# The four taps of a depthwise convolution: ScalarE multiplies, GpSimd adds, VectorE has no part, and the timetable is drawn up again

## The reference, cut to what matters

```python
h = x * rsqrt(mean(x * x) + EPS) * norm_scale
xs, res = split(h @ w_in, 2)
xs = silu(depthwise_conv(xs, conv_w) + conv_b)   # 4 taps, causal
delta, B, C = split(xs @ w_xproj, ...)
delta = softplus(delta @ w_dt + b_dt)
# scan over time for each of 16 states: h = exp(delta * A) * h + (delta * xs) * B
out = (y + xs * D) * silu(res)
```

## Time and profile before

| | us |
|---|---|
| median of 3 runs | 2735.68 |
| lowest and highest | 2731.32, 2737.05 |
| span of the profiled execution | 2733.1 |
| VectorE busy | 2470.7 (90%) |
| TensorE busy | 2233.0 (82%) |
| ScalarE busy | 1718.4 (63%) |
| GpSimd busy | 1638.1 (60%) |

### The profile page before, as it was taken

One profiled execution on the slowest core, in us unless ns is written; L12 is line 12 of the kernel. 1 busy time (PEld: TensorE's weight loads), 2 busy tenths in 40 slices (PEclk: granted clock), 3 DMA queues, 4 the chain that ended last, 5 costly groups with the idle time before them and its releaser, 6 DMA issues.

```text
span 2733.1 us, 35478 instructions
## 1 busy us (share of the span) xinstructions
PE 2233.0 (82%) x9268; PEld 1316.2 (48%) x9268; DVE 2470.7 (90%) x3315; ACT 1718.4 (63%) x3353; POOL 1638.1 (60%) x1083
## 2 busy tenths in 40 slices
PE   5666788888888888888888888888888888888798
PEld 2434355454544545454454545445454554545454
DVE  1699999999999999999999999999999999999951
ACT  3554675858567584766758476675847667584544
POOL 0667575757657575665757566575756757575610
PEclk9766899999999999999899998999999999999998
DMA  5011100101001010110101010010101001010100
GB/s 123 24 43 31 42 25 28 51 28 51 29 20 55 28 52 24 51 32 21 56 26 53 24 51 29 24 55 24 55 25 51 28 24 55 24 47 28 35 1 16
DMA packets 83410, 101.81 MB, mean 37 GB/s; under 512 B 23481, under 2 KB 49873, under 8 KB 83169
## 3 DMA queue, kind: packets, MB, share of 16 engines
q1 hardware_dynamic: 83168, 99.06, 12.2%
HBM read 90.13 MB, written 8.91 MB: 36 GB/s over the span
## 4 chain that ended last, share of the span: by engine, by line
DVE 37%; issue 27%; PE 14%; POOL 11%; ACT 5%; DVEq 1%; POOLq 0%; ACTq 0%
DVE h L1252 13%; DVE yT L1268 11%; PE bank L709 9%; POOL bx L680 7%; PE stateT L878 3%; DVE xs L1127 3%; DVE prod L1227 2%; ACT decay L1084 2%; ACT cum_sb L1049 2%; DVE res L1148 1%; DVE yT L1265 1%; POOL x_back L646 1%; DVE xs L1142 1%; PE bank L853 1%; DVE st L1107 1%
## 5 line engine op out<-in xcount | busy, mean ns | idle before, releaser
L680 POOL TENSOR_TENSOR bx<-dx,B_rows 128x1024 f32<-128x1024 f32 x512 | 1219.5, 2389 | 495.6 <-DVE h L1252 468.7
L1252 DVE TENSOR_TENSOR_SCAN h<-decay,bx 128x512 f32<-128x512 f32 x1024 | 1238.3, 1209 | 75.8 <-ACT decay L1084 52.0
L1084 ACT ACTIVATE decay<-delta,decay_rate 128x512 f32<-128x512 f32 x1024 | 706.8, 693 | 656.6 <-DVE h L1252 631.6
L878 PE MATMUL stateT<-ident,h 128*128 128x128 f32 x4096 | 683.6, 298 | 322.0 <-DVE h L1252 175.8
L878 PEld LDWEIGHTS stateT<-ident,h 128*128 128x128 f32 x4096 | 499.0, 150 | 725.5 <-issue 353.4
L1268 DVE SCALAR_TENSOR_TENSOR yT<-stateT,C_tok,yT 128x512 f32<-128x512 f32 x960 | 696.0, 725 | 16.3 <-PE stateT L878 16.0
L709 PE MATMUL bank<-q_to_expert,xnT 128*128 128x512 f32 x512 | 267.3, 649 | 12.5 <-ACT dx L988 12.4
L709 PE MATMUL bank<-k_to_expert,cumT 128*128 128x512 f32 x512 | 266.7, 647 | 9.3 <-DVE prod L1227 9.2
L709 PE MATMUL bank<-hT,w_in_sb 128*128 128x512 f32 x512 | 245.7, 610 | 18.1 <-DVE xs L1127 17.2
L1049 ACT ACTIVATE cum_sb<-bank,gate 128x64 f32<-128x64 f32 x1024 | 222.8, 329 | 39.4 <-PE bank L709 28.3
L853 PE MATMUL bank<-expert_to_out,prodT 128*128 128x256 f32 x1024 | 242.1, 379 | 0.4 <-ACT prodT L1059 0.4
(11 more groups left out here) (161 smaller groups left out, 2493.1 us busy)
## 6 DMA issues: line engine op xcount, KB each, us to landing
B_rows<-B_scratch SPq DMA_DIRECT2D x256, 256.0 KB, 3.2
x_front<-in_L_attn_x SPq DMA_DIRECT2D x16, 512.0 KB, 4.5
x_back<-in_L_attn_x SPq DMA_DIRECT2D x16, 512.0 KB, 5.1
out<-x_back SPq DMA_DIRECT2D x16, 512.0 KB, 3.3
w_in_sb<-in_L_attn_w_in SPq DMA_DIRECT2D x1, 1024.0 KB, 5.7
h<-in_L_ffn_V_fwd SPq DMA_DIRECT2D x2, 256.0 KB
h<-in_L_ffn_W_inv_exp SPq DMA_DIRECT2D x2, 256.0 KB
h<-in_L_ffn_W_fwd SPq DMA_DIRECT2D x2, 256.0 KB
```

What stands on the lines that cost most here:

```text
L680: pool.tensor_tensor(bx[use % BX_RING][:, :, :], dx[q.parity][:, 2 * half:2 * half + 2, :], row, ALU.mult).then_inc(s_bx.step(f"{n},{half} ...
L878: last = pe.transpose(stateT[j % 2][:, c * P:(c + 1) * P], h[n % 2][:, c, j * P:(j + 1) * P], ident[:, :])
L1084: act.activation(decay[c % 2][:, :], delta[q.parity][:, c, :], ACT.Exp, scale=decay_rate[:, c, n:n + 1]).then_inc(s_exp.step(f"{n},{c}"), 1)
L1252: dve.tensor_tensor_scan(h[n % 2][:, c, :], decay[c % 2][:, :], bx[(2 * n + c // 2) % BX_RING][:, c % 2, :], 0.0, ALU.mult, ALU.add).then_ ...
```

## The change

The three VectorE taps are gone. ScalarE, after its first product with the bias, writes three more products out of the same bank into `scratch` (task `tap`, at the same beats as `xs`), in a ring of four tiles: product p >= 4 waits for the addition of product p - 4. GpSimd adds them to `xs[c]` one after another (task `cv`, 12 additions a sequence, beats 38, 41, 43 and 52). The bank is free after the third product. The users of `scratch` and SiLU wait for GpSimd's last addition. The timetable is drawn up again; the rows below are those that move most or that the text names.

```diff
 TIMETABLE = {
-    ("F", "ag", "dve"): (8,),
-    ("F", "rs", "pool"): (15,),
-    ("F", "h", "act"): (17,),
-    ("F", "hT", "pe"): (17, 26),
-    ("F", "hT", "act"): (28, 31),
+    ("F", "ag", "dve"): (7,),
+    ("F", "rs", "pool"): (18,),
+    ("F", "h", "act"): (19,),
+    ("F", "hT", "pe"): (20, 28),
+    ("F", "hT", "act"): (29, 30),
-    ("F", "xs", "pe"): (32, 35, 37, 40),
+    ("F", "xs", "pe"): (29, 32, 34, 37),
     ("F", "xs", "act"): (34, 36, 40, 43),
-    ("F", "cvA", "dve"): (35, 37, 38, 42),
-    ("F", "cvB", "dve"): (37, 37, 39, 42),
-    ("F", "cvC", "dve"): (37, 37, 39, 44),
-    ("F", "res", "pe"): (36, 38, 41, 65),
+    ("F", "tap", "act"): (34, 36, 40, 43),
+    ("F", "cv", "pool"): (38, 41, 43, 52),
+    ("F", "res", "pe"): (35, 41, 41, 65),
...
-    ("B", "u", "dve"): (263, 264, 264, 268),
-    ("B", "o", "dve"): (268, 270, 271, 271),
-    ("B", "wo", "pe"): (274, 278, 282, 287),
-    ("B", "r", "dve"): (283, 283, 287, 289),
+    ("B", "u", "dve"): (263, 264, 267, 268),
+    ("B", "o", "dve"): (268, 268, 269, 270),
+    ("B", "wo", "pe"): (278, 280, 282, 287),
+    ("B", "r", "dve"): (284, 287, 288, 289),
...
     ("B", "rb", "pool"): (300,),
-    ("B", "t", "act"): (302,),
+    ("B", "t", "act"): (301,),
     ("B", "x1", "dve"): (301,),
...
-    ("B", "rb1", "pool"): (309,),
+    ("B", "rb1", "pool"): (314,),
...
-    ("L", "rs", "pool"): (473,),
+    ("L", "rs", "pool"): (468,),
...
-                return {"hT": (f_act, f"hT{k}"), "xs": (f_dve, f"cvC{k}"), "res": (f_act, f"res{k}"),
+                return {"hT": (f_act, f"hT{k}"), "xs": (f_act, f"tp{k}3"), "res": (f_act, f"res{k}"),
...
+            def conv_task(b, c, use):
+                pool.wait_ge(f_act.sem, f_act.done(b, f"cv{c}"))
+                for back in range(1, TAPS):
+                    product = 3 * c + back - 1
+                    pool.wait_ge(f_act.sem, f_act.done(b, f"tp{c}{back}"))
+                    if back > 1:
+                        pool.wait_ge(f_pool.sem, f_pool.done(b, f"cv{c}{back - 1}"))
+                    pool.tensor_tensor(xs[b.parity][:, c, back:], xs[b.parity][:, c, back:], scratch[:, product % 4, 0:T - back],
+                                       ALU.add).then_inc(f_pool.step(f"cv{c}{back}"), 1)
...
+            def tap_task(b, c, use):
+                act.wait_ge(f_pe.sem, f_pe.done(b, f"xs{c}"))
+                for back in range(1, TAPS):
+                    product = 3 * c + back - 1
+                    if product >= 4:
+                        before = product - 4
+                        act.wait_ge(f_pool.sem, f_pool.done(b, f"cv{before // 3}{before % 3 + 1}"))
+                    elif product == 0 and b.shift(-1).exists:
+                        act.wait_ge(f_dve.sem, f_dve.done(b.shift(-1), "d13"))
+                        if b.shift(-3).exists:
+                            act.wait_ge(b_pe.sem, b_pe.done(b.shift(-3), "lg"))
+                    act.activation(scratch[:, product % 4, 0:T - back], use.bank[:, 0:T - back], ACT.Copy,
+                                   scale=conv_w_sb[:, c, TAPS - 1 - back:TAPS - back]).then_inc(f_act.step(f"tp{c}{back}"), 1)
...
             def silu_task(b, k, use):
-                act.wait_ge(f_dve.sem, f_dve.done(b, "cvC3"))
+                act.wait_ge(f_pool.sem, f_pool.done(b, "cv33"))
...
-            def tap(back, name, before):
-
-                def task(b, c, use):
-                    x_c = xs[b.parity][:, c, :]
-                    dve.wait_ge(before[0].sem, before[0].done(b, f"{before[1]}{c}"))
-                    dve.scalar_tensor_tensor(out=x_c[:, back:], in0=use.bank[:, 0:T - back], scalar=conv_w_sb[:, c, TAPS - 1 - back:TAPS - back],
-                                             in1=x_c[:, back:], op0=ALU.mult, op1=ALU.add).then_inc(f_dve.step(f"{name}{c}"), 1)
-                return task
...
             def keep_task(b, k, use):
+                dve.wait_ge(f_pool.sem, f_pool.done(b, "r1"))
```

More of the change, by code:

```diff
@@ L104 @@
     ("F", "proj", "pe"): (75,),
[L105 to L106 removed]
+    ("F", "proj", "act"): (78,),
+    ("F", "B", "sp"): (70,),
     ("F", "Ct", "pe"): (94,),
[L108 removed]
+    ("F", "Ct", "act"): (98,),
     ("F", "dt", "pe"): (82, 89, 100, 108),
[L110 to L111 removed]
+    ("F", "dt", "act"): (90, 93, 107, 115),
+    ("F", "ex", "act"): (91, 94, 107, 117),
     ("F", "ln", "act"): (92, 96, 107, 119),
@@ L128 @@
     ("B", "ag1", "dve"): (304,),
-    ("B", "rb1", "pool"): (309,),
-    ("B", "xn", "act"): (310,),
+    ("B", "rb1", "pool"): (314,),
+    ("B", "xn", "act"): (316,),
     ("B", "xnT", "pe"): (317, 319),
-    ("B", "xnT", "act"): (320, 320),
-    ("B", "cum", "dve"): (322, 324),
+    ("B", "xnT", "act"): (320, 322),
+    ("B", "cum", "dve"): (322, 322),
     ("B", "rt", "pe"): (324, 327, 329, 333),
-    ("B", "rt", "act"): (331, 332, 332, 338),
+    ("B", "rt", "act"): (326, 328, 331, 337),
     ("B", "gelu", "act"): (338,),
-    ("B", "logit", "pe"): (342,),
@@ L138 @@
[L138 to L149, removed]
+    ("B", "logit", "pe"): (340,),
+    ("B", "logit", "act"): (344,),
+    ("B", "logit_rows", "pe"): (342,),
@@ L150 @@
+    ("B", "lb", "dve"): (344,),
+    ("B", "mx", "dve"): (345,),
+    ("B", "sub", "dve"): (345,),
+    ("B", "ex", "act"): (346,),
+    ("B", "sm", "dve"): (347,),
+    ("B", "sn", "dve"): (349,),
+    ("B", "rc", "dve"): (350,),
+    ("B", "wa", "dve"): (352,),
+    ("B", "gT", "pe"): (370,),
+    ("B", "gT", "act"): (377,),
     ("L", "cum", "pe"): (348, 354, 363, 374, 386, 390, 398, 428),
-    ("L", "xv", "pe"): (351, 358, 367, 378, 394, 423, 426, 431),
+    ("L", "xv", "pe"): (355, 358, 367, 378, 394, 423, 426, 431),
@@ L152 @@
     ("L", "cum", "act"): (357, 360, 368, 379, 391, 392, 408, 432),
[3 rows of a table removed]
[3 rows of a table added]
     ("L", "out", "pe"): (373, 381, 393, 398, 431, 434, 439, 443),
-    ("L", "out", "act"): (382, 401, 440, 445),
+    ("L", "out", "act"): (386, 401, 443, 445),
     ("L", "st", "dve"): (454,),
     ("L", "ag", "dve"): (462,),
-    ("L", "rs", "pool"): (473,),
-    ("L", "t", "act"): (468,),
-    ("F", "dx", "pool"): (105, 113, 126, 127),
+    ("L", "rs", "pool"): (468,),
+    ("L", "t", "act"): (470,),
+    ("F", "dx", "pool"): (105, 110, 126, 127),
@@ L163 @@
     ("L", "x", "pool"): (477, 477),
-    ("L", "store", "sp"): (466,),
+    ("L", "store", "sp"): (464,),
 }
-FILLED_BY = {("F", "hT"): "hT", ("F", "xs"): "xs", ("F", "cvA"): "xs", ("F", "cvB"): "xs", ("F", "cvC"): "xs", ("F", "res"): "res",
+FILLED_BY = {("F", "hT"): "hT", ("F", "xs"): "xs", ("F", "tap"): "xs", ("F", "res"): "res",
              ("F", "proj"): "proj", ("F", "Ct"): "Ct", ("F", "dt"): "dt", ("B", "u"): "y", ("B", "r"): "wo", ("B", "xnT"): "xnT",
@@ L731, in res_task @@
             def res_task(b, c, use):
+                if c == 0:
+                    pe.wait_ge(f_act.sem, f_act.done(b, "hT1"))
+                    if use.sem is f_act.sem:
+                        pe.sem_inc(passed["pe"], 1)
                 pe.wait_ge(use.sem, use.free_at)
@@ L1013, in rt_task @@
                         act.wait_ge(f_dve.sem, f_dve.done(b.shift(1), "d13"))
+                    if b.shift(2).exists:
+                        act.wait_ge(f_pool.sem, f_pool.done(b.shift(2), "cv33"))
                 act.wait_ge(b_pe.sem, b_pe.done(b, f"rt{k}"))
@@ L1084, in scan_part @@
                 act.activation(decay[c % 2][:, :], delta[q.parity][:, c, :], ACT.Exp, scale=decay_rate[:, c, n:n + 1]).then_inc(s_exp.step(f"{n},{c}"), 1)
-            walk(act, "act", prologue, {("F", "h"): h_task, ("B", "t"): t_task, ("B", "xn"): xn_task, ("L", "t"): out_centre, ("F", "hT"): hT_task, ("F", "xs"): xs_task, ("F", "res"): res_task, ("F", "silu"): silu_task,
+            walk(act, "act", prologue, {("F", "h"): h_task, ("B", "t"): t_task, ("B", "xn"): xn_task, ("L", "t"): out_centre, ("F", "hT"): hT_task, ("F", "xs"): xs_task, ("F", "tap"): tap_task, ("F", "res"): res_task, ("F", "silu"): silu_task,
                                  ("F", "proj"): proj_task, ("F", "Ct"): Ct_task, ("F", "dt"): dt_task, ("F", "ex"): ex_task, ("F", "ln"): ln_task, ("B", "xnT"): xnT_task, ("B", "rt"): rt_task,
```

20 lines of the change are left out of this document (9 added, 11 removed), and 6 rows, old and new, of the table TIMETABLE.

## The result

The changed kernel takes 2637.19 us (median of 4 runs, 2632.95 to 2640.34) where the kernel before, on the same chip, takes 2735.01 (2731.32 to 2737.05): a ratio of 0.9645, 95% interval 0.963 to 0.9659. It is faster by 97.8 us, more than twice the 40 us forecast, and lies 3 us under the low end of the range. The profiled execution has a span of 2638.5 us against 2733.1.

The account below looks back on a forecast made before the run. VectorE's own work bounds the steady period, plus 3.4 us of waits. Per period 8.06 + 2.4 - 7.35 = 3.1 us, 40 us over thirteen periods, total -40: median 2695 us (-1.5%), range 2640 to 2748.

Parts of the forecast that it names:

- The taps: Twelve taps of a sequence leave VectorE in beats 35 to 44, worth 8.06 us a period.
- The relief of `o_task`: Beats 12 to 15: with `rs` behind a `bx`, VectorE's four products get 2.4 us cheaper a period; bounds 0 and 2.7.
- The relief fails: Rival, chance 0.24: `o_task` still meets a `bx`; 0.7 us a period, 2727 us, near no change.
- the new wait: VectorE waits up to `x1` (beat 45): 7.35 us a period, near bounds 6.2 and 8.5.
- the chain up to `x1`: Slots 3 to 5: nine GpSimd additions, `bx`, `rb`, then ScalarE's `t` delay `x1` from 23.9 to 30.1, 6.2 us.
- the collision of `x1`: Beat 45: `x1` may have to wait for GpSimd's next `bx`, losing 2.3 us; half counted, 1.15.
- the price of the addition: One 512-element addition on GpSimd takes 1.35 us; bounds 1.27 and 1.70.
- The places of the waits: Beats 31 and 37 wait 1.3 and 3.0 us for TensorE, beat 44's scan for `bx`; longest wait at `x1` on `t`.
- The rest is nothing: Elsewhere the timetable moves by a beat or two, counted as nothing; 3.4 us of old waits stay.
- TensorE at half its clock: Rival, chance 0.19: `wo` 1, `wo` 2 and `xs` 0 run at 1.2 GHz, 1.7 us more each; 2762 us.
- Mostly hidden: Rival, chance 0.15: only TensorE limits in slots 3 to 5, wait 2.5 us, 8.0 gained a period; 2632 us.
- The early periods: First scanned period wins nothing, second 1.5 us; ahead of the first scan GpSimd's additions end some 1.5 us later.

Follow-up runs that it names:

- experiment 1: Changed kernel with only `rs` on GpSimd put back from beat 18 to 15, ahead of its `bx`: 2676.61 us, ratio 0.9789.
- after: The changed kernel itself, with the taps on ScalarE and GpSimd and the new order: 2637.19 us, ratio 0.9645.
- Experiment 12: Changed kernel with second `hT`, its copies and first `xs` earlier, third block's additions and fourth `xs` later, one `res` moved to beat 60: 2632.64 us.
- experiment 5: Changed kernel with half of the `xs` and `res` matmuls left out: 2611.24 us, ratio 0.9547.
- Experiment 13: Changed kernel with only the router's steps put back on the beats of the kernel before: 2640.27 us, ratio 0.965.
- experiment 3: Changed kernel's new order with the three tap steps back on VectorE at their old beats: 2759.49 us, ratio 1.0094.
- experiments 4 to 6: Changed kernel with two of three additions a block left out (2625.38 us), half the `xs` and `res` matmuls left out (2611.24), both cuts together (2550.68).

## Why the prediction came out too small

**What bounds.** Right that a microsecond taken from VectorE counts only while the others follow. VectorE's busy time fell to 2273 us, under the 2300 to 2340 forecast, mostly by the router's products.

**The taps.** 8.06 us forecast, 8.07 measured.

**The relief of `o_task`.** 2.4 forecast, 2.63 measured, and `rs` behind the `bx` did what was said (mean near 0.7: 0.677). *The relief fails* is out. Its worth was underrated all the same: experiment 1 loses 39 us, since TensorE is held up too and one `wo` runs at a lower clock.

**The step that failed: the new wait, 7.35 us in the sum and 4.84 measured.** It had two parts, the chain up to `x1` (6.2) and the collision of `x1` (1.15), and both were too large.

**The chain: the price of the addition.** I took 1.35 us for each of nine, with 1.27 as the lower bound. Three in a row take 3.57 from start to start (1191.43 to 1195.00), 1.19 each, below the lower bound. The single steps are 1.35, 1.17 and 1.04. So 1.35 was right for the first, which the second waits for; the second and third are 1.09 long where no addition of before was under 1.25, and that is 1.1 us of the nine; and the instruction behind the third does not wait for it, which is the rest. The earlier trace rows had another trap. The mean of 1.38 is no price of an addition alone:

```profile
L636 POOL TENSOR_TENSOR scratch<-scratch,dx x64: 1257/1274/1827, 70.7 to 2459.4; 128x512 f32<-128x512 f32 x64
```

The three numbers are least, median and most: 49 of the 64 take 1.29 us or less, 15 take 1.59 to 1.83, and in after, at other moments, the same addition has a mean of 1.28.

The Trainium skill, GPSIMD Engine Reference, section 3.1, gave 1.12 as an estimate of its figure; the mean of all 192 is 1.149, so the page was nearer than the rows I had, partly by luck, since no 512-element addition of this trace is that short. Its section 4.1 leaves elementwise work to VectorE; the price agrees in direction (1.19 for the addition alone where VectorE's whole tap took 0.67), but as advice it doesn't hold for this kernel, where GpSimd had the time. Nine additions are 1.4 us shorter than counted. They started at 9.4 instead of 9.2, the third block waited 0.43 us for its products, and VectorE's own work up to `x1` was 24.35 instead of 23.9 us. So `x1` starts at 29.2 instead of 30.1, and the wait is 4.84 instead of 6.2.

**The collision of `x1`.** 1.15 us counted as half a loss; the loss was nought, because `x1` came 0.13 us before the second `bx`, and GpSimd waited. That was luck: the prediction could not tell. Experiment 12 shows the loss to be real in another order: 1.2 us.

**The places of the waits.** Forecast at beats 31 and 37 for TensorE, 1.3 and 3.0: measured 1.53 and 1.60, and 0.48 later. `x1` on `t`: there, but 1.24 us and not the longest. The wait of the scan of beat 44 on `bx` did not come: the `bx` ended at 1207.25, the scan started at 1207.48. TensorE had held VectorE back just enough, and experiment 5, which frees TensorE, brings that wait out at 2.06 us.

**"The rest is nothing".** Not right: a term put at nothing. The router's products and `keep` gave 2.24 us, `gate` 0.21, other waits took 0.94 and small lengthenings 0.85, which leaves 0.66 a period. Experiment 13 shows that the products' 2.0 us are worth no time: the waits answer to them.

**TensorE at half its clock.** It did not happen to the three tasks named. The granted clock averages 0.57 in the window, lower than the 0.65 of before, but it fell on small work: two `stateT` tasks take 1.11 us instead of 0.60, a transpose of `x_front` 1.06, and the first two `wo` have 1.96 and 1.89. TensorE's gaps ahead of them were 1.12, 0.52 and 1.12 us. It was the order that spared the large tasks: in experiment 1 the first `wo` took 2.73 us, and in experiment 3 two large tasks took 3.50 and 3.41 instead of 1.88, behind gaps of 3.47 and 3.48 us and at clocks of 0.57 and 0.59. The Trainium skill, TensorE: Matmul & The Clock Gate, section "Why this matters for your kernels", warns of idle gaps between bursts of matmuls; the trace of experiment 3 agrees.

```profile
1178.58 1.11 PE L890 MATMUL stateT<-ident,h 128*128 128x128 f32 x4
1179.48 1.96 PE L717 MATMUL bank<-w_out_sb,res 128*128 128x256 f32 x8
1181.56 0.66 PE L890 MATMUL stateT<-ident,h 128*128 128x128 f32 x4
1182.05 1.89 PE L717 MATMUL bank<-w_out_sb,res 128*128 128x256 f32 x8
```

**Mostly hidden** came nearest in time (2632), by luck: it had a wait of 2.5 us and TensorE as the only limit. Both chains limit (experiments 4 to 6), and the wait was 4.8; other terms and the early periods made up for most of the difference.

**The early periods.** The first scanned period gained 3.7 us and the second 4.1, where I had 0 and 1.5. In the first VectorE's own time falls by 9.8 us and its waits grow by 6.0, in the second by 13.9 and 9.8: the waits took back most of it and not all. Up to the first accumulation 0.6 us are lost, not 1.5.

**The sum.** Forecast 3.1 us a period. The wait gives 7.35 - 4.84 = 2.51 more, `o_task` 0.23, the rest 2.24 + 0.21 - 0.85 - 0.94 = 0.66: 3.1 + 2.51 + 0.23 + 0.66 = 6.5, as measured. The miss of 58 us is three quarters the wait, 1.36 us of it the chain and 1.15 the collision. The walk of the four engines through the stretch found most of the places and the sign; what it lacked was a price for the addition that could be trusted within 0.15 us, since nine of them stood in one chain.

**Open.** Why the second and third addition of a block take 1.09 us and the first 1.27 (they differ by one or two elements, by what stands before them, and by where the row starts) was not tried. Nor was a price for each other step of the new order. Experiment 13 shows that the router's own beats make its products cheap, and that it is worth nothing there.

## What to carry to other kernels

Moving work off the busiest engine gives only as much as the other engines' chains let through in the very beats that it leaves: here 8.1 us of work left a period and the move alone gave 11 us of 2734, until the order of the streams was made anew for it. So test the move and the new order together and apart: -11, +25 and -98 show that neither can be judged by itself. When a wait stays after one chain is cut, look for a second of the same length, and cut both to know (-12, -26, -86.5). And before counting a relief, ask who is late next: 2.0 us of products a period were worth nothing here, while one step of `rs` was worth 39 us. Before a mean goes into a chain nine times, look at its spread: the 1.38 us of the earlier trace rows was 1.27 in three cases of four and 1.6 to 1.8 in the rest.
